# First cross-attention of a decoder on Trainium2: the 65-key tail becomes a seventh score chunk, and two chunks move behind the transposed maxima

## The reference, cut to what matters

```python
q_r = jnp.einsum('bshq,hqr->bhsr', q_big, W_qr)
k_r = jnp.einsum('bld,hdr->bhlr', kv_r, W_kr)
scores = jnp.einsum('bhsr,bhlr->bhsl', q_r, k_r)
attn = jax.nn.softmax(scores, axis=-1)
ctx_c = jnp.einsum('bhsl,bld->bhsd', attn, kv_r)
```

## Time and profile before

| quantity | value |
|---|---|
| median of 3 runs | 1365.95 us (1364.26 to 1366.72) |
| span of the profiled execution, its only time on the page | 1379.6 us |
| PE busy | 1272.7 us (92%) |
| POOL busy | 824.0 us (60%) |
| DVE busy | 868.2 us (63%) |
| ACT busy | 634.6 us (46%) |

### The profile page before, as it was taken

One profiled execution on the slowest core, in us unless ns is written; L12 is line 12 of the kernel. 1 busy time (PEld: TensorE's weight loads), 2 busy tenths in 40 slices (PEclk: granted clock), 3 DMA queues, 4 the chain that ended last, 5 costly groups with the idle time before them and its releaser, 6 DMA issues.

```text
span 1379.6 us, 20358 instructions
## 1 busy us (share of the span) xinstructions
PE 1272.7 (92%) x7123; PEld 826.8 (60%) x7123; DVE 868.2 (63%) x1490; ACT 634.6 (46%) x1687; POOL 824.0 (60%) x748
## 2 busy tenths in 40 slices
PE   7999997999999999999999758998999999989792
PEld 4865554666666666666668643445776874556582
DVE  4756666677777777778865636675666123664443
ACT  3731123445554455544551416887665115872151
POOL 1267005799999999999993445887444004560444
PEclk9999997999999999999999888999999997998897
DMA  9501111000000000000005620000000105200263
GB/s 261 134 9 32 37 31 27 9 8 9 9 11 10 9 9 9 10 11 9 9 5 176 195 65 2 1 1 1 1 1 1 27 1 155 63 1 32 69 142 118
DMA packets 66172, 58.91 MB, mean 43 GB/s; under 512 B 19424, under 2 KB 62968, under 8 KB 65560
## 3 DMA queue, kind: packets, MB, share of 16 engines
q1 hardware_dynamic: 62952, 49.09, 12.7%
q0 software_dynamic: 3120, 8.52, 2.6%
HBM read 40.69 MB, written 8.52 MB: 36 GB/s over the span
## 4 chain that ended last, share of the span: by engine, by line
PE 79%; DVE 6%; ACT 5%; POOL 4%; issue 4%; DMA 1%; DVEq 0%; SPq 0%; POOLq 0%; ACTq 0%
PE PS L515 73%; PE PS L523 5%; ACT s_sc L1402 2%; POOL a_m L2137 2%; POOL a_m L2131 2%; DVE s_mx L1859 1%; ACT a_m L1356 1%; DVE pm L1622 1%; DVE HN L1504 0%; PE PS L729 0%; DMA f_xg<-token_rows,f_ids 0%; POOL s_sc L2152 0%; PE PS L685 0%; POOL f_xg L2119 0%; PE PS L623 0%
## 5 line engine op out<-in xcount | busy, mean ns | idle before, releaser
L2080 POOL TENSOR_TENSOR PWS<-PWS 128x1024 f32<-128x1024 f32 x160 | 379.7, 2373 | 45.1 <-ACT PWS L1286 25.8
L1622 DVE TENSOR_REDUCE pm<-PS 128x2 f32<-128x1024 f32 x192 | 225.8, 1218 | 69.3 <-PE PS L515 68.7
L1286 ACT ACTIVATE PWS<-PS 128x512 f32<-128x512 f32 (+1 forms) x416 | 213.3, 599 | 78.4 <-PE PS L515 78.2
L515 PE MATMUL PS<-PWS,KVR 128*64 128x256 f32 (+1 forms) x1664 | 185.8, 380 | 0.0
L515 PE MATMUL PS<-QALL,KH 128*128 128x512 f32 (+1 forms) x416 | 182.6, 439 | 0.9 <-DVE QM L1646 0.9
L515 PE MATMUL PS<-QM,KL 68*128 68x512 f32 (+1 forms) x416 | 167.3, 402 | 0.0
L2152 POOL TENSOR_SCALAR s_sc<-s_sc,s_ri 128x128 f32<-128x128 f32 (+1 forms) x256 | 104.5, 429 | 98.9 <-DVE s_ri L1866 98.9
L515 PEld LDWEIGHTS PS<-PWS,KVR 128*64 128x64 f32 (+1 forms) x1664 | 121.4, 137 | 59.0 <-issue 0.9
L515 PEld LDWEIGHTS PS<-QALL,KH 128*128 128x128 f32 (+1 forms) x416 | 77.9, 187 | 76.9 <-ACT PWS L1286 57.4
L1402 ACT ACTIVATE s_sc<-PS,s_nb 128x128 f32<-128x128 f32 (+1 forms) x256 | 104.5, 433 | 3.9 <-DVE s_nb L1862 3.9
L1859 DVE TENSOR_REDUCE s_mx<-PS 128x2 f32<-128x512 f32 (+2 forms) x112 | 65.7, 611 | 50.1 <-PE PS L515 50.0
(11 more groups left out here) (328 smaller groups left out, 2518.3 us busy)
## 6 DMA issues: line engine op xcount, KB each, us to landing
QALL<-qlo SPq DMA_DIRECT2D x32, 128.0 KB, 2.4
QM<-QALL SPq DMA_DIRECT2D x64, 64.0 KB, 2.0
f_w<-in_L_ffn_w_dram SPq DMA_DIRECT2D x2, 2048.0 KB
tile_results<-e_y SPq DMA_DIRECT2D x31, 128.0 KB
a_nat<-in_L_attn_w_qkv_dram SPq DMA_DIRECT2D x1, 3072.0 KB, 13.0
x_wq<-in_L_xattn_Wq_dram SPq DMA_DIRECT2D x1, 2048.0 KB, 10.4
x_wo<-in_L_xattn_Wo_dram SPq DMA_DIRECT2D x2, 1024.0 KB, 6.9
a_wo<-in_L_attn_w_o_dram SPq DMA_DIRECT2D x1, 2048.0 KB, 17.5
```

The source lines that it names most:

```text
L515: return nc.tensor.matmul(o, a, b, start=start, stop=stop, **kw)
L1286: nc.scalar.activation(PW[c][0:rows, j * HALF:(j + 1) * HALF], st_bank("block", LT * u + lt)[0:rows, :], ACT.Exp).then_inc(p_ready, 1)
L1622: V.tensor_reduce(pm[u % 2][:, :, i // 3, i % 3], src, AX, ALU.max).then_inc(nat_read, 1)
L2080: G.tensor_tensor(ACC[:, :], PW[0][:, :] if i == 0 else ACC[:, :], PW[i + 1][:, :], ALU.add).then_inc(acc_step, 1)
```

## The change

The tail becomes the fifth of seven chunks of a unit (`PLAINS = 7`, `TAIL = 4`). Its four matmuls now take 64 rows each, head by head, and write into the two pairs of banks of the plain chunks. It no longer has a place in the ring of three banks, nor semaphores of its own. The middle group is now tail, chunk, chunk; the late and after groups keep two chunks each. On PE the late group moves from ahead of the transposed maxima to behind the transposed maxima and keys, ahead of the sums. On DVE `maximum_rows` and `keys` move ahead of the late maxima. `turned_scores` takes over a wait of unit 0 that stood in the tail.

```diff
-        PLAINS = 6
+        PLAINS = 7
+        TAIL = 4
...
-                    for a, z in ((4, 6), (6, 8), (8, 10))]
-
-        ST_ITEMS = [("tail", 0), ("maxima", 0)]
+                    for a, z in ((4, 7), (7, 9), (9, 11))]
+
+        def plain_part(n):
+
+            u, i = divmod(n, PLAINS)
+            return u, None if i == TAIL else i - (i > TAIL)
+
+        ST_ITEMS = [("maxima", 0)]
         for u in range(UNITS):
-            ST_ITEMS += [("block", LT * u + lt) for lt in (FRONT if u else range(LT))]
-            ST_ITEMS += [("tail", u + 1)] if u + 1 < UNITS else []
-            ST_ITEMS += [("block", LT * u + lt) for lt in (BACK if u else ())]
+            ST_ITEMS += [("block", LT * u + lt) for lt in range(LT)]
...
                 if n >= 2:
                     pe.wait_ge(nat_read, n - 1)
+                if i is None:
+                    plain_tail(n, b, p)
+                    return
...
+            def plain_tail(n, b, p):
+
+                if p == 0:
+                    pe.wait_ge(rows_set, 2 if b else 1)
+                    pe.wait_ge(*(kl_ready, 4 * b) if b else banks.emptied(("k", 3)))
+                for st in range(2):
+                    for h in range(2):
+                        last = mm(plain_banks(n)[:, h * 512 + st * 256:h * 512 + st * 256 + 66],
+                                  QALL[h * D:(h + 1) * D, p, b, h, st * P:(st + 1) * P],
+                                  KH[b % 2][h * D:(h + 1) * D, 3 * HALF:3 * HALF + 66])
+                last.then_inc(nat_full, 1)
...
-                ps = st_begin("tail", u)
...
-                for h in range(2):
-                    for st in range(2):
-                        a = h * 256 + st * P
-                        last = mm(ps[:, a:a + 66], QALL[:, p, b, h, st * P:(st + 1) * P], KH[b % 2][:, 3 * HALF:3 * HALF + 66])
-                last.then_inc(tail_full, 1)
...
             for n in range(PLAINS):
                 plain_scores(n)
-            plain_tail(0)
             turn_maxima(0)
...
-                if u + 1 < UNITS:
-                    plain_tail(u + 1)
                 for n in middle:
                     plain_scores(n)
                 if u > 0:
-                    turned_scores(u, BACK)
-                for n in late:
-                    plain_scores(n)
+                    turned_scores(u, RUNS[1])
                 if u + 1 < UNITS:
                     turn_maxima(u + 1)
                 if keys_due(u):
                     keys(*keys_due(u))
+                for n in late:
+                    plain_scores(n)
                 if u >= 1:
                     weight_sums(u - 1)
                 context(u, range(LT))
...
             def maxima(n):
 
-                u, i = divmod(n, PLAINS)
+                u, i = plain_part(n)
                 dve.wait_ge(nat_full, n + 1)
                 if i == 0 and u >= 2:
                     dve.wait_ge(mx_ready, u - 1)
+                if i is None:
+                    src = plain_banks(n).rearrange("p (h s c) -> p h s c", h=2, s=2)[:, :, :, 0:LREST]
+                    V.tensor_reduce(pm[u % 2][:, :, :, 3], src, AX, ALU.max).then_inc(nat_read, 1)
+                    return
...
                 for n in middle:
                     maxima(n)
                 if u + 1 < UNITS:
                     all_maxima(u + 1)
-                for n in late:
-                    maxima(n)
-                if u + 1 < UNITS:
                     maximum_rows(u + 1)
                 if keys_due(u):
                     keys(*keys_due(u))
+                for n in late:
+                    maxima(n)
                 if u >= 1:
                     normalised(u - 1)
```

More of the change, by code:

```diff
@@ L390, in decoder @@
         nat_read = sem("plain_scores_reduced")
-        tail_full = sem("plain_tails_filled")
-        tail_read = sem("plain_tails_reduced")
         mx_ready = sem("query_maxima_ready")
@@ L427, in decoder @@
         CHUNKS = 7
-        PLAINS = 6
+        PLAINS = 7
+        TAIL = 4
         ADDS = 7
-        FRONT, BACK = range(0, 6), range(6, LT)
+        RUNS = (range(0, 6), range(6, LT))
         CTX_BANK = PS[:, 7 * 512:8 * 512]
@@ L478, in st_freed @@
             return {"keys": lambda: (kl_ready, 4 * (at_[0] - 1) + at_[1] + 1), "maxima": lambda: (qm_ready, at_[0] + 1),
-                    "block": lambda: (p_ready, at_[0] + 1), "tail": lambda: (tail_read, at_[0] + 1),
+                    "block": lambda: (p_ready, at_[0] + 1),
                     "sums": lambda: (norm_done, at_[0] + 1)}[kind]()
@@ L705, in plain_scores @@
                 last.then_inc(nat_full, 1)
[L707 to L714, removed]
-                ps = st_begin("tail", u)
-                if p == 0 and b > 0:
-                    pe.wait_ge(rows_set, 2)
-                    pe.wait_ge(kl_ready, 4 * b)
-                for h in range(2):
-                    for st in range(2):
-                        a = h * 256 + st * P
-                        last = mm(ps[:, a:a + 66], QALL[:, p, b, h, st * P:(st + 1) * P], KH[b % 2][:, 3 * HALF:3 * HALF + 66])
-                last.then_inc(tail_full, 1)
+            def plain_tail(n, b, p):
[8 more added lines that the diff above has]
+                last.then_inc(nat_full, 1)
             def turn_maxima(u):
@@ L733, in turned_scores @@
                 b, p = divmod(u, PAIRS)
-                if blocks is FRONT:
+                if blocks[0] == 0:
                     pe.wait_ge(qh_moved[u % 2], 32 * (u // 2 + 1))
                     pe.wait_ge(qm_ready, u + 1)
+                if u == 0 and blocks[0] == 0:
+                    pe.wait_ge(*banks.emptied(("q", PAIRS - 1, 1)))
+                    pe.wait_ge(rows_set, 1)
+                    for s in range(2):
+                        pe.wait_ge(q_moved[s], 32 * PAIRS)
                 for lt in blocks:
@@ L771, in _ @@
                 middle, late, after = plains_after(u)
-                turned_scores(u, FRONT)
+                turned_scores(u, RUNS[0])
                 if u == 0:
@@ L775, in _ @@
                         plain_scores(n)
-                    turned_scores(0, BACK)
+                    turned_scores(0, RUNS[1])
                     for n in range(PLAINS + 2, PLAINS + AHEAD):
                         plain_scores(n)
-                if u + 1 < UNITS:
-                    plain_tail(u + 1)
                 for n in middle:
@@ L1302, in _ @@
             for u in range(UNITS):
-                weights(u, FRONT)
-                weights(u, BACK)
+                weights(u, range(LT))
                 if keys_due(u):
@@ L1620, in maxima @@
                     dve.wait_ge(mx_ready, u - 1)
+                if i is None:
+                    src = plain_banks(n).rearrange("p (h s c) -> p h s c", h=2, s=2)[:, :, :, 0:LREST]
+                    V.tensor_reduce(pm[u % 2][:, :, :, 3], src, AX, ALU.max).then_inc(nat_read, 1)
+                    return
                 src = plain_banks(n).rearrange("p (h c) -> p h c", h=2)
                 V.tensor_reduce(pm[u % 2][:, :, i // 3, i % 3], src, AX, ALU.max).then_inc(nat_read, 1)
[L1624 to L1630, removed]
             def all_maxima(u):
                 dve.wait_ge(nat_read, PLAINS * (u + 1))
-                dve.wait_ge(tail_read, u + 1)
                 if u >= 2:
@@ L1677, in _ @@
                 maxima(n)
-            tail_maxima(0)
             all_maxima(0)
@@ L1684, in _ @@
                 middle, late, after = plains_after(u)
-                if u + 1 < UNITS:
-                    tail_maxima(u + 1)
                 for n in middle:
```

## The result

The changed kernel takes 1384.94 us (median of 4 runs, 1380.98 to 1385.20) beside 1366.05 us for the kernel before (4 runs): a ratio of 1.0139, interval 1.0112 to 1.0167. That is 18.9 us more where 14.0 were forecast.

The account below looks back on a forecast made before the run. PE was taken to bound the phase, as long as POOL (15.36 us a round) keeps up. The terms 9.3 - 0.4 + 4.0 + 0.6 + 0.5 = 14.0 us, added to the median 1365.95, gave 1380 us, range 1369 to 1387.

Parts of the forecast that it names:

- both mechanisms: PE's third middle chunk waits for DVE's tail reduction; in key units the first transposed key waits for ACT's exponentiation.
- The middle group: Block 5's last matmul to block 6's load: 1.69 us against 1.38, 0.31 more in each of 30 units, 9.3 us.
- The end of a unit without keys: Block 12's second matmul to the sums' load: 1.17 us against 1.19, 0.02 less in 18 units, 0.4 us.
- The keys: End of 11 key units: transposed keys wait for ACT to read block 11, 0.36 us more each, 4.0 us.
- The start: Unit 0, paced by DVE, with the tail between fourth and fifth chunk: 0.6 us more, between 0 and 0.8.
- The seven units with one more subtraction: Units 24 to 30: the tail's reduction adds to the load's wait, 0 to 0.15 us each, 0.5 us in all.
- The tail is reduced in time: Middle group: the tail is released 0.33 us behind its first load; 1365 us, no change; chance 0.08.
- Neither wait is met: Middle group and keys: PE gets at both loads without the release counted on; about 5 us less, 1361 us; chance 0.07.
- Two heads at once bring the tail nothing: Middle group: the tail's four loads still run one behind the other, 6.6 us more, 1386.5 us; chance 0.08.

Follow-up runs that it names:

- `tail_only`: The kernel after with the late group put back ahead of the transposed maxima, on PE and DVE: 1380.62 us, ratio 1.0114.
- the two runs on the reduction's length: The kernel after with DVE's reduction of the tail done twice, 1391.94 us, and with it reading 8 of the tail's 65 keys, 1373.40 us.
- `order_only`: The kernel before, tail still in the ring, with the late group behind the transposed maxima and keys, on PE and DVE: 1368.46 us, ratio 1.0049.
- `keys_last`: The kernel after with the order maxima, late group, keys on both engines: 1376.02 us, ratio 1.0097.
- the pair: Two later profiled executions within 1 us of their kernels' medians: the kernel before unchanged at 1365.07 us, the kernel after unchanged at 1384.61 us.
- `tail_ring2`: The kernel before with the tail as two items of the ring of three, one a head, both behind the middle chunks: 1359.58 us, ratio 0.9966.
- `before_again`: The kernel before, unchanged, run once more for a second profile: 1365.07 us.
- `after_timed`: The kernel after, unchanged, in five rounds against the kernel before: 1385.50 us against 1364.56, ratio 1.0143; its profiled execution took 1384.61 us.
- `after_again`: The kernel after, unchanged, run once more for a second profile: 1370.54 us.

## Why the prediction held, and where its sum was off

Forecast 1380 us, between 1369 and 1387; measured 1384.94. The direction and both mechanisms are as it put them, and the total is 4.9 us short.

**The middle group** was forecast at 1.69 us by 0.32 + 0.93 + 0.44. Over the 24 units 1 to 24 of the after trace the median is 1.689. DVE starts 0.454 us behind the tail's first load (forecast 0.45), PE loads 0.053 behind the end of the reduction (0.05), and the third chunk loads 0.937 behind the first (0.93). `tail_only` gives 0.31 a unit, and the two runs on the reduction's length show it to be the cause.

**The end of a unit without keys** was put at 0.02 us less; `order_only` has 0.04 less. **The keys** were put at 0.36 us more, by a first key 0.79 us behind block 12's last matmul. Unit 8 after:

```profile
365.64 0.40 PE L517 MATMUL PS<-QM,KL 68*66 68x512 f32 x1
...
366.44 0.63 PE L687 MATMUL PS<-ident,DUP 128*128 128x128 f32 x4 [0.22 <-ACT PWS L1287]
...
367.66 0.20 PEld L517 LDWEIGHTS PS<-WS,ones 128*64 128x64 f32 x4 [0.37 <-issue]
```

0.80 us, and 2.02 to the sums where 1.98 were forecast. The sentence that gave the whole 0.36 to the uncovered wait was too simple: `keys_last` gets back only 0.24 by covering it.

**The start** was put at 0.6 us: from DVE's first reduction to the first transposition it is 9.68 us in all three profiles of after, 9.10 and 9.09 before.

**The seven units with one more subtraction** were put at 0.5 us more. This term was wrong in sign. Unit 26 after, DVE's and the loader's rows of the timeline:

```profile
649.80 2.34 DVE L1626 TENSOR_REDUCE pm<-PS 128x2 f32<-128x1024 f32 x2
652.15 0.43 DVE L1623 TENSOR_REDUCE pm<-PS 128x4 f32<-128x260 f32 x1
...
651.70 0.30 PEld L517 LDWEIGHTS PS<-KH,QALL 64*128 64x128 f32 x4 [0.37 <-issue]
652.19 0.18 PEld L517 LDWEIGHTS PS<-KH,QALL 64*128 64x128 f32 x2 [0.20 <-DVE pm L1626]
652.64 0.19 PEld L517 LDWEIGHTS PS<-KH,QALL 64*128 64x128 f32 x2 [0.26 <-DVE pm L1623]
```

The wait for the after chunks lies inside the 0.94 us from the tail's first load to the third chunk's, which PE waits anyway. These units take 15.82 us like the others, while before they took 0.08 us more than the others on average.

So between transposition 2 and 31 the terms gave 29 x 0.31 - 0.4 + 4.0 + 0.5 = 13.1 us, and 12.1 were measured; the microsecond is that last term, which is 0.5 less instead of 0.5 more. The start and the phase together are 13.4 us longer in the pair (0.6 and 12.8). **The step that was off is the sum's silent one:** it lets everything outside the phase stand as it was. In the pair that represents the medians the part behind the phase is 6.9 us longer, by TensorE's granted clock (last section).

How much of the 18.9 us is the clock's can be read from the runs themselves, since each has a mean granted clock, as a share of 2.4 GHz, on record beside its time. Times in us of runs with the same mean clock:

| mean granted clock | before | after |
|---|---|---|
| 0.967 | 1356.63, 1356.77 | 1370.54 |
| 0.958 | 1362.48, 1364.56, 1365.84 | 1380.98 |
| 0.951 to 0.952 | 1369.96, 1370.41, 1370.53, 1370.84 | 1384.28, 1384.61, 1384.90, 1385.74, 1387.59 |

Over the 50 runs of before that ran beside the experiments and the 11 of after, one straight line of time against clock for both kernels puts them 14.4 us apart, with a standard error of 0.6. So at an equal clock the change costs about what the sum says, 14.0, and the other 4.5 us of the medians go with the clock: its median is 0.960 in the runs of before and 0.954 in those of after. That 1384.94 still lies inside the range is partly luck: it stands at the top of the forecast's own 1373 to 1385, and the room there was meant for larger terms in the units, not for another stage.

**The rivals.** "The tail is reduced in time" fell by the 0.454 us until DVE starts. "Neither wait is met" fell by the two brackets. "Two heads at once bring the tail nothing" fell too: six loads stand in 0.41 us, two steps of 0.11 and a load of 0.19, so that each pair of the tail takes one step. (The rival's case that the steps are as long as a load was misread: a load lasts 0.19 us and the next starts 0.11 behind it.) The Trainium skill, TensorEngine Tiling (Array Packing), section Performance Considerations, says not to take a tiling factor out of a dimension that is already small. The prediction applied that to the tail, whose columns are few; but the 66 columns are not what is divided, the 128 rows are. So the rule does not make the rival's case, and the trace shows the opposite outcome: pairing the heads takes two steps instead of four. `tail_ring2`, which also has the tail behind the two chunks, gains 0.21 us a unit; what that place is worth by itself was not run. What lost the time is where the results were put. On that the Trainium skill, Perfetto Trace Analysis, section Optimizing Tensor Performance, has matmul groups rotate through different banks, so that one is read out beside the next. The trace agrees, and adds the depth: two pairs of banks did that for two items in a row and not for three.

## What to carry to other kernels

An item that joins a rotation can cost a wait as soon as more items stand in a row than there are buffers: count from the first load to the reader's release, and compare that with the time until the buffer comes round again. A cheap item is no exception, since most of the 0.94 us here is matmul to reader to release, and less than half is the reading. Before work is moved off a place, look what wait it was covering there (here ACT's, ahead of the keys); and where a gain in PE steps is right but the banks are wrong, keep the first and change the second, as `tail_ring2` does.

## What was not expected of the hardware

**A stretch at half clock whose length changes between executions.** The score matmuls of the second cross-attention start about 435 us behind the last transposition of the changed phase, with the same instructions in all kernels. Their group (`y_km`, `y_q`), with 533 ns as the mean of one, in `before_again`:

```profile
L515 PE MATMUL PS<-y_km,y_q 32*128 32x256 f32 (+1 forms) x128 | 29.2, 533 | 0.0
```

and in `after_timed`:

```profile
L517 PE MATMUL PS<-y_km,y_q 32*128 32x256 f32 (+1 forms) x128 | 32.9, 593 | 0.0
```

The windows from the 10th to the 30th microsecond of that stage; the third number from the end is the granted clock. First `before_again`:

```profile
1158.54:1168.54 10.00, 9.74 (x96) 5.12 (x88) 6.76 (x20) 7.48 (x33) 5.84 (x16) 0.96 0.31 78
1168.54:1178.54 10.00, 9.48 (x95) 4.91 (x94) 6.88 (x22) 8.44 (x36) 6.11 (x16) 1.00 0.01 2
```

then `after_timed`:

```profile
1170.62:1180.62 10.00, 10.00 (x60) 4.79 (x54) 4.52 (x13) 5.58 (x26) 4.68 (x12) 0.50 0.05 17
1180.62:1190.62 10.00, 10.00 (x54) 4.81 (x53) 3.87 (x12) 4.41 (x18) 3.25 (x8) 0.55 0.01 2
```

In one PE is back at 2.4 GHz in the first of them; in the other it stays at 1.2 GHz, busy throughout, and does 114 matmuls where the first does 191. All twelve profiled executions fall into two groups by the mean of that matmul: five with 533 to 548 ns, which take 649.5 to 651.5 us from the last transposition to the end, and seven with 582 to 611 ns, of which six take 657.7 to 661.9. The seventh is the first profile of before with 669.9, which loses some ten more in the last expert stage. So the stretch alone is worth some 8 us. What PE does just before does not tell the two apart. In the first profiles and in the `_again` profiles of both kernels the first 8 us of the stage look alike: at full clock PE is busy all of the first 4 us, then 1.15 to 1.16 us of the next 2, then 0.97 to 0.98 of 2 while the clock falls to 0.50 (in `after_timed` it falls some 2 us sooner). In both `_again` profiles it is back 12 us into the stage, in both first ones 28 us into it. Both kernels show both kinds: of before one profile in two is long, of after two in three.

**The first two units of the phase** do something like it: 37.8 to 38.6 us in four executions, 34.4 to 35.9 in the others. The window from 225 to 245 us shows the clock, in `before_again`:

```profile
225.00:245.00 20.00, 18.68 (x61) 10.83 (x61) 11.12 (x12) 6.43 (x11) 14.33 (x7) 0.51 0.03 7
```

and in `after_again`:

```profile
225.00:245.00 20.00, 15.86 (x93) 9.06 (x92) 11.17 (x13) 4.36 (x10) 12.64 (x7) 0.83 0.03 7
```

The Trainium skill, TensorE: Matmul & The Clock Gate, section "What's actually happening", says that the moment at which the clock changes varies from run to run, as what watches the activity isn't started by the kernel. The page puts that variation at half a microsecond either way. These executions agree that the moment varies, but not with the size: the stretch in the second cross-attention differs by some 8 us, so the measurement decides. No run here shows the cause.

**Left open:** why the kernel after had the long stretch in nearly all of its runs. Its times are 1380.98 us and above but for one of 1370.54, while before spread from 1356 to 1370 beside it. That its arrival in that stage is shifted against something is a guess that no run here tested. So the 12.8 us of the phase are shown with their cause, and what lies beyond the sum is placed and tied to the granted clock, but why the clock is lower in runs of after stays open.
